# The edge stage of a graph network kernel by pairs of tiles, with ScalarE making the one-hots from distances

## The chip, the cores and the metric

One core of a Trainium2 chip runs the program. The metric is the device time of one execution in microseconds (us); lower is better. The kernel before was run three times in the series shown here, and one further execution was profiled.

## The reference, cut to what matters

```python
h = relu(layernorm(x))                       # x: 3125 nodes, 256 features
msg_input = concat([h[src], h[dst], edge_attr])   # 50000 edges, sorted by dst; 16 edge features
hid = relu(msg_input @ mW1 + mb1)            # 512 wide
messages = hid @ mW2 + mb2
aggregated = segment_sum(messages, src)      # per source node
x = x + h + (relu(concat([h, aggregated]) @ uW1 + ub1) @ uW2 + ub2)
# then three graph convolutions over the same edges, with degree norms and self loops
```

Since the sum over edges is linear, the kernel sums `hid` per source node first and multiplies by `mW2` afterwards. With A = h @ mW1[0:256] + mb1 and B = h @ mW1[256:512], the hidden row of an edge is relu(A[src] + B[dst] + edge_attr @ mW1[512:528]).

## The kernel before, in words

There are four stages with a barrier between them. `sort_and_embed` groups the edges by blocks of 128 source nodes and writes them to a list in DRAM (`src_list`), computes A (kept in SBUF, as an upper and a lower part of 512 columns a block) and B (written to DRAM). `edge_mlp` is the edge stage. `build_and_update` builds the count matrix C and updates the nodes, and `graph_layers` does the three convolutions.

The list is cut into NT = 440 tiles of 128 edges. Tiles come in PAIRS = 220 pairs; both tiles of a pair belong to one block of source nodes, so the sums of a pair go to one place. Each engine runs its own written-out loop in order, and semaphores connect them. For tile t of the edge stage:

- SyncE (line 937) loads the list's rows, four tiles at a time, into a ring of four such groups.
- GpSimd copies the indices of four tiles (line 946) and gathers the 128 rows of B of a tile with an indirect DMA (line 949), up to eight tiles ahead of VectorE's addition.
- VectorE makes the one-hot `oh` (line 1031): iota equal to the edge's source within the block, 128 wide, float32r.
- TensorE turns the one-hot and the edge features (`turn`, lines 963 and 964, bf16).
- ScalarE copies the turned one-hot to SBUF and sums it along the row into `tile_deg` (line 1009, with a read of the accumulator), and copies the turned edge features (line 1011).
- TensorE adds three products of 512 columns into PSUM (`edge`, lines 971 and 973): edge features times weights, and the turned one-hot times the two parts of A, which picks A[src]. Where A is read depends on the pair's block, whose offset comes from a register.
- VectorE adds the gathered rows of B (`pre`, line 1040).
- ScalarE applies relu (line 1018). An even tile is written in float32 as `hid_whole`. An odd tile is written in float32r as `hid_upper`, and VectorE makes the rest, `hid_lower` = max(pre, 0) - upper (line 1046).
- TensorE multiplies the one-hot into the pair's sum (`node`): line 987 for a whole tile, lines 983 and 985 for the upper and lower part of a split tile.
- VectorE adds the pair's result onto the sums of its block (line 1055), or begins new ones, with `going_on` as the factor.

TensorE's loop does turn(t), edge(t-1), node(t-3); ScalarE's turn copies of t, relu of t-1; VectorE's one-hot of t+1, addition of t-2, lower part of t-3 and, each second time, a pair's sum. The block offsets are loaded into registers (line 72) every four pairs, on TensorE and on VectorE, where the group has five values, as the sum also reads at the previous pair's offset. In `build_and_update`, the degree sums of 440 tiles are turned in four blocks of 128 (lines 1217 and 1318) and multiplied with weights `tile_w` that say to which block a tile belongs (line 1334).

## Time and profile before

| | us |
|---|---|
| median of three runs | 2326.61 (2321.5 to 2326.86) |
| the profiled execution, its own time | 2330.37 |
| its span, first to last instruction | 2328.6 |
| the edge stage in it | 684.0 to 1404.5 |

Busy times over the span are TensorE 1882.8 us (81%), VectorE 1575.9 (68%), GpSimd 1255.4 (54%) and ScalarE 823.2 (35%), and the mean granted clock of TensorE is 0.885 of full speed.

A busy time is the time in which an engine had an instruction in it; register, branch and semaphore instructions are not counted. PE is TensorE, PEld its weight load, DVE VectorE, ACT ScalarE, POOL GpSimd, SP SyncE; a q behind the name is the engine's sequencer. "idle before" is the time for which an engine stood still ahead of an instruction, with what released it; "issue" is time for which the profile shows no releaser. L1040 is line 1040 of the kernel before.

### The profile page before, as it was taken

How to read it: one execution, taken by the hardware profiler on the slowest of the kernel's cores; microseconds unless marked ns; L12 is line 12 of the kernel's file. 1: busy time of each engine (PE TensorE's matmuls, PEld its weight loads, DVE VectorE, ACT ScalarE, POOL GpSimd, SP SyncE). 2: the span in 40 equal slices, each digit the busy share in tenths (PEclk: the TensorE clock that was granted, in tenths of full speed). 3: DMA queues.
4: the chain of work that ended last, by engine and by line, in shares of the span. 5: the costliest groups of instructions: out<-in, count | busy, mean ns of one | idle time of the engine just before them, and what ended most of it. 6: DMA issues, size and time to landing. Idle time of an engine off the chain costs nothing. (4 is left out here: it accounts for less than half of the span.)

```text
span 2328.6 us, 36393 instructions
## 1 busy us (share of the span) xinstructions
PE 1882.8 (81%) x8866; PEld 1281.5 (55%) x8866; DVE 1575.9 (68%) x4877; ACT 823.2 (35%) x2533; POOL 1255.4 (54%) x1508
## 2 busy tenths in 40 slices
PE   3354656455448999999999998999997999999998
PEld 2222323232225555555555555777675788788786
DVE  7665656465448999999989997787777535335333
ACT  0111111111115666666666664555556012112000
POOL 3566665665656666666666656999887500000000
PEclk7576676666659999999999998999998999999999
DMA  4011111111126666666666684111115333333333
GB/s 137 26 41 37 39 44 35 41 33 42 34 65 173 183 180 180 183 180 181 186 171 184 184 161 129 61 59 59 59 64 152 94 109 115 103 109 120 97 109 96
DMA packets 179413, 247.68 MB, mean 106 GB/s; under 512 B 28860, under 2 KB 146937, under 8 KB 179210
## 3 DMA queue, kind: packets, MB, share of 16 engines
q0 software_dynamic: 47888, 126.25, 19.8%
q1 hardware_dynamic: 99730, 93.08, 13.2%
q10 hardware_dynamic: 31592, 26.02, 3.4%
q8 instruction: 81, 1.33, 0.2%
q14 instruction: 122, 1.00, 0.2%
HBM read 199.08 MB, written 46.09 MB: 105 GB/s over the span
## 5 line engine op out<-in xcount | busy, mean ns | idle before, releaser
L366 POOL DMA_INDIRECT src_list<-ring,ring_row x392 | 405.7, 1035 | 263.4 <-DVE ring L584 148.9
L949 POOL DMA_INDIRECT brow<-B_rows,rows x440 | 421.4, 958 | 230.6 <-DVE pre L1040 150.2
L1822 PE MATMUL pO<-F,y 128*128 128x512 f32 x1728 | 437.9, 407 | 10.7 <-DVE y L1642 6.5
L1822 PEld LDWEIGHTS pO<-F,y 128*128 128x128 f32 x1728 | 327.8, 190 | 90.4 <-DVE y L1642 6.8
L973 PE MATMUL pEdge<-A,turned 128*128 x880 | 362.7, 494 | 0.0
L1040 DVE TENSOR_TENSOR pre<-pEdge,brow 128x512 f32<-128x512 f32 x440 | 301.5, 685 | 44.1 <-PE pEdge L973 21.8
L1186 POOL TENSOR_SCALAR src_oh<-iota,src_s 128x128 bf16<-128x128 bf16 x473 | 303.2, 656 | 32.6 <-PE pC L1357 30.5
L791 PE MATMUL pP<-U,upto 128*128 128x182 bf16 x385 | 61.3, 327 | 296.8 <-DVE posf L554 292.3
L791 PEld LDWEIGHTS pP<-U,upto 128*128 128x128 bf16 x385 | 44.8, 130 | 335.2 <-DVE posf L554 312.4
L987 PE MATMUL pNode<-hid_whole,oh 128*128 128x512 f32 x440 | 229.1, 602 | 0.0
L1018 ACT ACTIVATE hid_upper<-pre 128x512 fp32r<-128x512 f32 x220 | 138.7, 631 | 243.2 <-DVE pre L1040 195.3
L1638 DVE CAST F<-raw 128x512 fp32r<-128x512 uint16 x432 | 173.7, 438 | 66.4 <-PE pO L1822 60.6
L971 PE MATMUL pEdge<-we_rows,turned_e 96*128 96x512 bf16 x440 | 170.7, 388 | 40.7 <-ACT turned_e L1011 34.7
L1230 DVE TENSOR_SCALAR dst_oh<-iota_cw,dst_s 128x458 bf16<-128x458 f16 x568 | 182.8, 374 | 0.7 <-PE pC L1357 0.4
L1055 DVE SCALAR_TENSOR_TENSOR sums<-sums,going_on,pNode 128x512 f32 x220 | 163.2, 742 | 27.1 <-issue 26.8
L973 PEld LDWEIGHTS pEdge<-A,turned 128*128 128x128 f32 x880 | 171.5, 195 | 11.9
L554 DVE CUSTOM_DVE_ANT_0 junk<-pP,U 128x182 bf16<-128x182 f32 x392 | 109.2, 339 | 100.6 <-remote 95.6
L1357 PE MATMUL pC<-dst_oh,src_oh 128*128 128x458 bf16 x568 | 157.6, 362 | 14.9 <-SPq L1304 6.0
L1046 DVE SCALAR_TENSOR_TENSOR hid_lower<-pre,hid_upper 128x512 fp32r<-128x512 f32 x220 | 149.8, 681 | 0.8 <-ACT hid_upper L1018 0.7
L1442 ACT CAST c_rows<-pC 128x458 uint16<-128x458 f32 x175 | 94.6, 541 | 155.6 <-PE pC L1357 138.7
L1018 ACT ACTIVATE hid_whole<-pre 128x512 f32<-128x512 f32 x220 | 139.2, 633 | 16.3 <-DVE pre L1040 5.5
L513 DVE TENSOR_SCALAR U<-bin_iota,bin_f 128x182 bf16<-128x182 bf16 x392 | 76.9, 284 | 89.8 <-remote 89.6
(284 smaller groups left out, 3257.2 us busy)
## 6 DMA issues: line engine op xcount, KB each, us to landing
raw<-C_rows SPq DMA_DIRECT2D x72, 768.0 KB, 4.4
C_rows<-c_rows ACTq DMA_DIRECT2D x175, 114.5 KB, 1.7
rows<-src_list SPq DMA_DIRECT2D x110, 100.0 KB
brow<-B_rows,rows POOLq DMA_INDIRECT x440
B_rows<-bst SPq DMA_DIRECT2D x25, 256.0 KB
src_list<-ring,ring_row POOLq DMA_INDIRECT x392
hT_rows<-A SPq DMA_DIRECT2D x25, 128.0 KB
resid<-in_x_dram SPq DMA_DIRECT2D x1, 3072.0 KB
```

The lines of the kernel that those rows point to most:

```text
L366: nc.gpsimd.indirect_dma_start(dr.src_list[:, :, :].rearrange("p t w -> (p t) w"), bass.IndirectOffsetOnAxis(ap=ring_row[:, k % RING, t:t ...
L949: nc.gpsimd.indirect_dma_start(brow[:, t % BR, :], None, dr.B, bass.IndirectOffsetOnAxis(ap=rows_i[:, b, j, 1:2], axis=0)).then_inc(b_in[t ...
L971: mm(pE[t % 2][:, :], turned_e[:, t % 2, :], keep.we[:, :], start=True, stop=False)
L973: last = mm(pE[t % 2][:, :], turned[:, t % 2, :], keep.A[:, 2 * HID + k * HID:][:, bass.ds(at[t // 2], HID)], start=False, stop=(k == 1))
L987: last = mm(pN[p % 2][:, :], oh[:, t % OHS, :].bitcast(F32), whole[(t % 4 + 1) // 2][:, :], start=first, stop=not first)
L1018: nc.scalar.activation(to, pre[:, u % 2, :], ACT.Relu).then_inc(hid_ready, 1)
L1040: v.tensor_tensor(pre[:, t % 2, :], pE[t % 2][:, :], brow[:, t % BR, :], ALU.add).then_inc(pre_ready, 1)
L1055: v.scalar_tensor_tensor(out=keep.sums[:, bass.ds(at[p], HID)], in0=keep.sums[:, bass.ds(at[max(p - 1, 0)], HID)], scalar=keep.going_on[:, ...
L1186: nc.gpsimd.tensor_scalar(src_oh[:, s % SLOTS, :], keep.iota16[:, :], src_s[:, s:s + 1], None, ALU.is_equal).then_inc(src_ready, 1)
L1230: v.tensor_scalar(dst_oh[:, s % SLOTS, :], iota_cw[:, :], dst_s[:, s:s + 1], None, ALU.is_equal).then_inc(dst_ready, 1)
L1638: v.tensor_copy(F[:, n % FS, :], raw[:, m % RAWS, n % RAWW, :]).then_inc(f_ready, 1)
L1822: last = mm(pO[m % 2][half][:, :], y[:, win, part, half * P:(half + 1) * P], F[:, n % FS, :], start=(win == 0 and part == 0), stop=False)
```

## The change

The edge stage goes by pairs. Each of TensorE's, ScalarE's and VectorE's steps handles two tiles.

- VectorE's one-hots are gone. ScalarE computes for each tile the distances |source - iota| (`distances`, Abs, bf16, 128 wide, two instructions a pair), two pairs ahead. From them it makes the one-hots of a pair as relu(1 - distance) in one instruction of 256 columns (`one_hots`). TensorE turns the distances rather than the one-hots, and ScalarE's copy of the turned ones applies relu(1 - distance) on the way (`turn_over`, 256 wide, its row sum going into `pair_deg`). The bias of Abs, and the one of both relus, is an operand of one value a partition.
- In every first (even) pair, as before, the first tile is whole and the second is split. In every second (odd) pair both tiles are split: ScalarE's upper and VectorE's lower part are then 1024 wide.
- VectorE's addition is one instruction of 1024 columns a pair, into a PSUM tile of two banks; SyncE and GpSimd wait for it by pairs.
- TensorE's loop does turn(i), edge(i-1), node(i-3) of pairs. node(p) waits for the sum of pair p-2 by `sums_ready`. ScalarE's does turn_over(i), distances(i+2), one_hots(i), relus(i-2); VectorE's add_target(i-1), lower_part(i-2), add_pair(i-4).
- The registers are loaded every eight pairs, eight values at a time, on both engines, on VectorE within add_pair.
- `build_and_update` has 220 degree sums, in two blocks, and computes the weights of pairs.
- The semaphores of the first stage's set-up are merged into one, `set_up`, in the order in which GpSimd counts it up.

The core of the diff; of the edge stage only the new lines and those that stay are shown:

```diff
...
+        LCS = 4
         BR = 8
+        GRP = 8
+        QUADS = NT // LC
+        OHR = 6
+        DR = 4
+        WHOLE, SPLIT = 2, 2
         rows = g.sb("rows", [P, LCS, LC, ROW])
         brow = g.sb("brow", [P, BR, HID])
+        apart = g.sb("apart", [P, DR, 2, P], BF16)
+        oh = g.sb("oh", [P, OHR, 2, P], F32R)
+        turned = g.sb("turned", [P, 2, 2 * P], F32R)
+        turned_e = g.sb("turned_e", [EW, 2, 2 * P], BF16)
+        pre = g.sb("pre", [P, 2, 2 * HID])
+        whole = g.sb("hid_whole", [P, WHOLE, HID])
+        upper = g.sb("hid_upper", [P, SPLIT, 2 * HID], F32R)
+        lower = g.sb("hid_lower", [P, SPLIT, 2 * HID], F32R)
         pT = [g.ps(f"pTurn{n}", [P, 2 * HID], BF16) for n in range(2)]
+        pE = [g.ps(f"pEdge{n}", [P, 2 * HID]) for n in range(2)]
         pN = [g.ps(f"pNode{n}", [P, HID]) for n in range(2)]
+        apart_ready = g.sem("apart_ready")
+        whole_ready = g.sem("whole_ready")
+        upper_ready = g.sem("upper_ready")
+        sums_ready = g.sem("sums_ready")
+        def both(p):
+            return p % 2 == 1
+        def first(p):
+            return 0 if both(p) else HID
+        def wholes(p):
+            return p - p // 2
         block = stack.enter_context(nc.Block())
         @block.sync
         def _(sp):
+            for m in range(QUADS):
                 if m >= LCS:
+                    sp.wait_ge(pre_ready, 2 * (m - LCS + 1))
                     sp.wait_ge(cols_copied, m - LCS + 1)
                 sp.dma_start(rows[:, m % LCS, :, :], dr.src_list[:, m * LC:(m + 1) * LC, :]
                              ).then_inc(rows_in[m % LCS], 16)
...
         @block.gpsimd
         def _(pool):
             for t in range(NT):
+                m, j = divmod(t, LC)
                 if j == 0:
+                    pool.wait_ge(rows_in[m % LCS], 16 * (m // LCS + 1))
+                    nc.gpsimd.tensor_copy(keep.cols[:, t:t + LC, :], rows[:, m % LCS, :, 0:2]).then_inc(cols_copied, 1)
                 if t >= BR:
+                    pool.wait_ge(pre_ready, (t - BR) // 2 + 1)
                 nc.gpsimd.indirect_dma_start(
                     brow[:, t % BR, :], None, dr.B,
+                    bass.IndirectOffsetOnAxis(ap=rows_i[:, m % LCS, j, 1:2], axis=0)).then_inc(b_in[t % BR], 16)
+            pool.wait_ge(cols_copied, QUADS)
         @block.tensor
         def _(pe):
             mm = nc.tensor.matmul
             at = blocks_of(nc, pe, keep.pair_at, 0, GRP)
+            def turn(p):
+                q, j = divmod(2 * p, LC)
+                pe.wait_ge(apart_ready, 2 * p + 2)
+                if p >= 2:
+                    pe.wait_ge(turn_copied, p - 1)
+                for n in range(2):
+                    nc.tensor.transpose(pT[p % 2][:, n * P:(n + 1) * P], apart[:, p % DR, n, :], keep.ident16[:, :])
+                for n in range(2):
+                    last = nc.tensor.transpose(pT[p % 2][0:EW, (2 + n) * P:(3 + n) * P],
+                                               rows16[:, q % LCS, j + n, 4:4 + EW], keep.ident16[:, :])
+                last.then_inc(turn_done, 1)
+            def edge(p):
+                pe.wait_ge(turn_copied, p + 1)
+                if p >= 2:
+                    pe.wait_ge(pre_ready, p - 1)
+                for n in range(2):
+                    to = pE[p % 2][:, n * HID:(n + 1) * HID]
+                    mm(to, turned_e[:, p % 2, n * P:(n + 1) * P], keep.we[:, :], start=True, stop=False)
+                    for k in range(2):
+                        last = mm(to, turned[:, p % 2, n * P:(n + 1) * P],
+                                  keep.A[:, 2 * HID + k * HID:][:, bass.ds(at[p], HID)], start=False, stop=(k == 1))
                 last.then_inc(edge_done, 1)
+            def node(p):
+                to = pN[p % 2][:, :]
+                pe.wait_ge(oh_ready, p + 1)
+                if p >= 2:
+                    pe.wait_ge(sums_ready, p)
+                if not both(p):
+                    pe.wait_ge(whole_ready, wholes(p) + 1)
+                    mm(to, oh[:, p % OHR, 0, :].bitcast(F32), whole[:, wholes(p) % WHOLE, :], start=True, stop=False)
+                pe.wait_ge(upper_ready, p + 1)
+                tiles = (0, 1) if both(p) else (1,)
+                for n in tiles:
+                    mm(to, oh[:, p % OHR, n, :], upper[:, p % SPLIT, n * HID:(n + 1) * HID],
+                       start=(both(p) and n == 0), stop=False)
+                pe.wait_ge(lower_ready, p + 1)
+                for n in tiles:
+                    last = mm(to, oh[:, p % OHR, n, :], lower[:, p % SPLIT, n * HID:(n + 1) * HID], start=False,
+                              stop=(n == 1))
                 last.then_inc(node_done, 1)
+            pe.wait_ge(sums_ready, 1)
+            for i in range(PAIRS + 3):
+                if i < PAIRS:
+                    turn(i)
+                if 0 <= i - 1 < PAIRS:
+                    edge(i - 1)
+                if 0 <= i - 3 < PAIRS:
+                    node(i - 3)
+                if i % GRP == 0 and 0 < i < PAIRS:
+                    at.update(blocks_of(nc, pe, keep.pair_at, i, min(GRP, PAIRS - i)))
         @block.scalar
         def _(act):
+            def distances(p):
+                q, j = divmod(2 * p, LC)
+                act.wait_ge(rows_in[q % LCS], 16 * (q // LCS + 1))
+                if p >= DR:
+                    act.wait_ge(turn_done, p - DR + 1)
+                    act.wait_ge(oh_ready, p - DR + 1)
+                for n in range(2):
+                    nc.scalar.activation(apart[:, p % DR, n, :], keep.iota[:, :], ACT.Abs,
+                                         bias=rows[:, q % LCS, j + n, 0:1], scale=-1.0).then_inc(apart_ready, 1)
+            def one_hots(p):
+                act.wait_ge(apart_ready, 2 * p + 2)
+                if p >= OHR:
+                    act.wait_ge(node_done, p - OHR + 1)
+                nc.scalar.activation(oh[:, p % OHR, :, :], apart[:, p % DR, :, :], ACT.Relu, bias=keep.ones[:, 0:1],
+                                     scale=-1.0).then_inc(oh_ready, 1)
+            def turn_over(p):
+                act.wait_ge(turn_done, p + 1)
+                if p >= 2:
+                    act.wait_ge(edge_done, p - 1)
+                nc.scalar.activation(turned[:, p % 2, :], pT[p % 2][:, 0:2 * P], ACT.Relu, bias=keep.ones[:, 0:1],
+                                     scale=-1.0, accum_out=keep.pair_deg[:, p:p + 1])
+                nc.scalar.copy(turned_e[:, p % 2, :], pT[p % 2][0:EW, 2 * P:4 * P]).then_inc(turn_copied, 1)
+            def relus(p):
+                act.wait_ge(pre_ready, p + 1)
+                if not both(p):
+                    if wholes(p) >= WHOLE:
+                        act.wait_ge(node_done, p - 2 * WHOLE + 1)
+                    nc.scalar.activation(whole[:, wholes(p) % WHOLE, :], pre[:, p % 2, 0:HID], ACT.Relu
+                                         ).then_inc(whole_ready, 1)
+                if p >= SPLIT:
+                    act.wait_ge(node_done, p - SPLIT + 1)
+                nc.scalar.activation(upper[:, p % SPLIT, first(p):2 * HID], pre[:, p % 2, first(p):2 * HID], ACT.Relu
+                                     ).then_inc(upper_ready, 1)
+            for p in range(2):
+                distances(p)
+            for i in range(PAIRS + 2):
+                if i < PAIRS:
+                    turn_over(i)
+                if i + 2 < PAIRS:
+                    distances(i + 2)
+                if i < PAIRS:
+                    one_hots(i)
+                if i >= 2:
+                    relus(i - 2)
         @block.vector
         def _(dve):
             v = nc.vector
+            v.memset(keep.sums[:, 0:HID], 0.0).then_inc(sums_ready, 1)
             at = {}
+            def add_target(p):
+                dve.wait_ge(edge_done, p + 1)
+                for t in (2 * p, 2 * p + 1):
+                    dve.wait_ge(b_in[t % BR], 16 * (t // BR + 1))
+                if p >= 2:
+                    dve.wait_ge(whole_ready, wholes(p - 1))
+                    dve.wait_ge(upper_ready, p - 1)
+                    dve.wait_ge(lower_ready, p - 1)
+                at_row = (2 * p) % BR
+                v.tensor_tensor(pre[:, p % 2, :], pE[p % 2][:, :],
+                                brow[:, at_row:at_row + 2, :].rearrange("p t n -> p (t n)"), ALU.add
+                                ).then_inc(pre_ready, 1)
+            def lower_part(p):
+                dve.wait_ge(upper_ready, p + 1)
+                if p >= SPLIT:
+                    dve.wait_ge(node_done, p - SPLIT + 1)
+                at_col = first(p)
+                v.scalar_tensor_tensor(out=lower[:, p % SPLIT, at_col:2 * HID], in0=pre[:, p % 2, at_col:2 * HID],
+                                       scalar=0.0, in1=upper[:, p % SPLIT, at_col:2 * HID].bitcast(F32), op0=ALU.max,
+                                       op1=ALU.subtract).then_inc(lower_ready, 1)
             def add_pair(p):
+                if p % GRP == 0:
+                    at.update(blocks_of(nc, dve, keep.pair_at, p, min(GRP, PAIRS - p)))
+                dve.wait_ge(node_done, p + 1)
+                dve.wait_ge(sums_ready, p + 1)
                 v.scalar_tensor_tensor(out=keep.sums[:, bass.ds(at[p], HID)],
                                        in0=keep.sums[:, bass.ds(at[max(p - 1, 0)], HID)],
                                        scalar=keep.going_on[:, p:p + 1], in1=pN[p % 2][:, :],
+                                       op0=ALU.mult, op1=ALU.add).then_inc(sums_ready, 1)
+            for i in range(PAIRS + 5):
+                if 0 <= i - 1 < PAIRS:
+                    add_target(i - 1)
+                if 0 <= i - 2 < PAIRS:
+                    lower_part(i - 2)
+                if 0 <= i - 4 < PAIRS:
+                    add_pair(i - 4)
+            dve.wait_ge(sums_ready, PAIRS + 1)
...
-            for m in range(KT):
-                link(v.tensor_scalar(ends_after[:, :], keep.tiles_end[:, 0:NW], part_m[:, m:m + 1], None, ALU.is_gt))
...
+            for m in range(KP):
+                link(v.tensor_scalar(pair_m[:, m:m + 1], keep.part[:, :], float(m * P), 2.0, ALU.add, ALU.mult))
+                link(v.tensor_scalar(ends_after[:, :], keep.tiles_end[:, 0:NW], pair_m[:, m:m + 1], None, ALU.is_gt))
+                v.tensor_copy(pair_w[:, m, 0:1], ends_after[:, 0:1]).then_inc(pair_w_ready, 1)
+                link(v.tensor_tensor(pair_w[:, m, 1:NW], ends_after[:, 1:NW], ends_after[:, 0:NW - 1], ALU.subtract))
...
+            for m in range(KP):
+                size = min(P, PAIRS - m * P)
+                last = mm(pX[:, 0:NW], degT[0:size, m, :], pair_w[0:size, m, :], start=(m == 0), stop=(m == KP - 1))
```

## Rows read from the trace of the kernel before

**Rows 1.** Busy time by stage: stretch, length, then each engine, clock, DMA share, GB/s
```profile
684.00:1404.50 720.50, 673.59 (x3080) 411.74 (x3080) 647.10 (x1321) 445.48 (x1760) 473.33 (x550) 0.98 0.64 177
```

**Rows 2.** The chain that ended last in order of time, first piece: start, us, what
```profile
1774.72 6.85 DMA raw<-C_rows
```

**Rows 3.** TensorE's order of time, one pair: start, us, engine, line, operation
```profile
1009.48 1.02 PE L987 MATMUL pNode<-hid_whole,oh 128*128 128x512 f32 x2
1010.33 0.22 PE L963 MATMUL pTurn<-ident,oh 128*128 128x128 bf16 x1
1010.39 0.22 PE L964 MATMUL pTurn<-ident,rows 128*96 128x128 bf16 x1
...
1011.13 0.39 PE L983 MATMUL pNode<-hid_upper,oh 128*128 128x512 f32 x1
...
1011.59 0.23 PE L963 MATMUL pTurn<-ident,oh 128*128 128x128 bf16 x1
```

**Rows 4.** The same view, whole node products at both ends of four pairs and between
```profile
1019.00 1.02 PE L987 MATMUL pNode<-hid_whole,oh 128*128 128x512 f32 x2
...
1025.03 1.05 PE L987 MATMUL pNode<-hid_whole,oh 128*128 128x512 f32 x2
...
1028.71 1.02 PE L987 MATMUL pNode<-hid_whole,oh 128*128 128x512 f32 x2
...
1031.64 1.02 PE L987 MATMUL pNode<-hid_whole,oh 128*128 128x512 f32 x2
```

**Rows 5.** VectorE's order of time, lower part and sum of two pairs
```profile
1007.17 0.68 DVE L1046 SCALAR_TENSOR_TENSOR hid_lower<-pre,hid_upper 128x512 fp32r<-128x512 f32 x1
1007.77 0.74 DVE L1055 SCALAR_TENSOR_TENSOR sums<-sums,going_on,pNode 128x512 f32 x1
...
1010.28 0.68 DVE L1046 SCALAR_TENSOR_TENSOR hid_lower<-pre,hid_upper 128x512 fp32r<-128x512 f32 x1
1011.45 0.75 DVE L1055 SCALAR_TENSOR_TENSOR sums<-sums,going_on,pNode 128x512 f32 x1 [0.49 <-issue]
```

**Rows 6.** VectorE's register loads, line 72, 1000 to 1050, then 684 to 702 us
```profile
L72 DVEq TENSOR_LOAD <-pair_at x4: 1180/1181/1183, 1010.0 to 1049.9; - x4
...
L72 DVEq TENSOR_LOAD <-pair_at x1: 594/594/594, 700.5 to 700.5; - x1
```

**Rows 7.** Groups by line and form, ScalarE then VectorE: busy us, mean ns, idle before
```profile
L1713 ACT ACTIVATE y<-h_g,dis 128x256 fp32r<-128x256 f32 x75 | 38.0, 509 | 21.6 <-PE pO L1822 19.6
...
L1747 ACT ACTIVATE h_g<-tmp 128x256 f32<-128x256 f32 x48 | 20.0, 416 | 132.9 <-DVE tmp L1664 132.9
...
L425 ACT ACT_TABLE_LOAD x1 | 1.3, 1283 | 0.0
...
L1257 DVE SCALAR_TENSOR_TENSOR sums<-mb,deg_src,pG 128x256 f32<-128x256 f32 x25 | 11.9, 475 | 7.9 <-PE pG L1367 7.9
```

**Rows 8.** ScalarE's order of time in the edge stage
```profile
1006.96 0.26 ACT L1009 ACTIVATE turned<-pTurn 128x128 fp32r<-128x128 bf16 x1
...
1007.21 0.25 ACT L1011 COPY turned_e<-pTurn 96x128 bf16<-96x128 bf16 x1
1007.36 0.63 ACT L1018 ACTIVATE hid_whole<-pre 128x512 f32<-128x512 f32 x1
1007.89 0.27 ACT L1009 ACTIVATE turned<-pTurn 128x128 fp32r<-128x128 bf16 x1
```

**Rows 9.** Groups by line, 700 to 1390 us: GpSimd's gathers
```profile
L949 POOL DMA_INDIRECT brow<-B_rows,rows x430 | 411.5, 957 | 228.0 <-DVE pre L1040 150.2 <-issue 77.8
```

**Rows 10.** All engines' order of time at the end of the stage
```profile
1402.11 0.69 DVE L1046 SCALAR_TENSOR_TENSOR hid_lower<-pre,hid_upper 128x512 fp32r<-128x512 f32 x1 [0.69 <-ACT hid_upper L1018]
...
1402.85 0.49 PE L985 MATMUL pNode<-hid_lower,oh 128*128 128x512 f32 x1 [0.23 <-DVE hid_lower L1046]
```

**Rows 11.** Groups by line, 1404 to 1425 us, VectorE then TensorE
```profile
L1217 DVE COPY degT<-pU 128x128 f32<-128x128 f32 (+1 forms) x4 | 0.9, 278 | 0.0
...
L1334 PE MATMUL pX<-tile_w,degT 128*128 128x25 f32 (+1 forms) x8 | 2.0, 392 | 1.7 <-DVE degT L1217 1.7
```

199 lines of the change are left out of this document (34 added, 165 removed).

## The prediction

> **What bounds the kernel now.** I first read the page and the busy times by stage: the change rewrites only the edge stage, from 684.0 to 1404.5 us, and there TensorE is busy 673.6, VectorE 647.1, GpSimd 473 and ScalarE 445 of 720.5 us [rows 1]. The chain of work that ended last starts at 1774.72 us [rows 2], after a barrier, so it says nothing of this stage; but all engines meet at its end, so what it gains or loses goes into the time in full. So I read its inner rhythm.
>
> TensorE's order of time is packed. The whole product takes 0.85 us (1009.48 to 1010.33), a tile's turn and edge products 0.80 (to 1011.13), the split product 0.46 (to 1011.59) [rows 3]. A pair is 2 x 0.80 + 0.85 + 0.46 = 2.91 us. From whole product to whole product one sees the real period: four pairs take 1031.64 - 1019.00 = 12.64 us, 3.16 a pair, where 4 x 2.91 is 11.64; of the 1.00 lost, 0.77 are in one pair, 1025.03 to 1028.71 [rows 4]. What lies there is VectorE's load of block offsets into registers: it takes 1.18 us, starting at 1010.0 in one group, and the sum behind it starts at 1011.45, 1.17 after the lower part's start, where a pair without a load has 0.60 (1007.17 to 1007.77) [rows 5, 6]. So TensorE is the bound, plus a hiccup each four pairs. The stage is 220 x 3.16 = 695.2 and 25.3 of start, end and rare stalls.
>
> **The change: what each engine has to do.** TensorE keeps four transposes and six edge matmuls a pair (2 x 0.80 = 1.60; each transpose takes 0.06 of it [rows 3]). Its node part is 0.85 + 0.46 = 1.31 in every first pair as now, and two split tiles, 0.92, in every second. Packed it would need 2.91 and 2.52, mean 2.72: the gain on offer is 0.19 x 220 = 42 us.
>
> VectorE loses its two one-hots (ScalarE makes them now), adds both targets in one instruction, and makes a lower part 1024 wide in every second pair. The slope is (0.74 - 0.475)/256 = 1.04 ns an element [rows 5, 7], so 512 more elements add 0.53: a 1024-wide one lets the next start after 1.13 us (bounds 1.06 and 1.20). Sum: 1.13 + (0.60 + 1.13)/2 + 0.74 = 2.74 us.
>
> ScalarE's present spacing is 0.25 for a 128-wide turn with its accumulator read, 0.15 for the edge features, and a 512-wide relu takes 0.63 and lets the next start after 0.53, 0.10 before its end [rows 8]. A 256-wide one with one pointer operand takes 0.509, without one 0.416: 0.093 for the pointer [rows 7]. The slope is (0.633 - 0.416)/256 = 0.85 ns. New, with a pointer in the first, third and fourth: turn 256 wide 0.25 + 0.11 + 0.09 = 0.45; features 0.15 + 0.11 = 0.26; two distances of 0.30; one-hots 0.41: 1.72 us. Relus: 0.53 + 0.53 in a first pair, 0.63 + 0.43 - 0.10 = 0.96 in a second. Mean 2.73 (bounds 2.5 without pointer cost, 2.9 with twice it).
>
> GpSimd is busy 473.3/220 = 2.15 us a pair [rows 1], and 77.8 us of gaps between its gathers, over some 215 pairs, wait for nothing that the profile shows [rows 9]: 0.36, together 2.51 at least. Its gathers keep eight tiles of lead and SyncE's loads of rows four groups of four; I cost both at nothing, covered while a pair takes over 2.5 to 2.7, and if that cover is gone VectorE's addition waits for gathers. Three engines are then within 0.02 of each other, and none bounds alone. The waits do.
>
> **The loop through the queues.** In ScalarE's new order the relus of pair i-2 stand behind the turn of pair i, though their input is long there. VectorE's lower part waits for them; the sum of pair i-4 is queued behind that lower part; TensorE's node product of pair i-2 waits for this sum (its PSUM bank); and the turn of pair i+2 is queued behind the node product. From turn i to turn i+2, pair i-2 a first (second) pair:
> - result visible 0.16 after the next could start (0.22 less 0.06 [rows 3]), start 0.02
> - ScalarE 1.72, then to the end of its upper part 0.53 + 0.63 = 1.16 (1.06)
> - to VectorE 0.05; lower part until the sum may start 0.60 (1.13); the sum 0.74 [rows 5]
> - to TensorE 0.05, as from 1402.11 + 0.69 to 1402.85, and 0.10 for weights that could not load ahead (0.49 against 0.39) [rows 3, 10]
> - node product 1.31 (0.92), turn 0.23
>
> That is 6.14 us (6.18) for two pairs, 3.08 a pair, over the packed 2.72: TensorE idles ahead of node products, and almost nothing of the 0.19 is left but what the hiccup gives back. VectorE fits in: it gets the edge result 1.56 after turn i, adds for 1.13, and is free at about 2.7 to 3.0, the lower part's inputs being there at 3.11.
>
> **The register loads.** VectorE's now come every eight pairs, of eight values instead of five. The first, of four, took 0.59 us and those of five 1.18 [rows 6], so they go by fours and eight cost 1.18 too. The load sits inside the loop: from its start to the sum is 1011.45 - 1010.0 = 1.45, against 0.60 [rows 5, 6]. That is 0.85 each eight pairs (bounds 0.3, if the other loop's idle absorbs it, and 1.5). TensorE's load stands behind a node product of 0.92 that hides it.
>
> Eight pairs: 4 x 6.14 + 0.85 = 25.4, 3.18 a pair; 220 x (3.18 - 3.16) = +4. Start and end: the first addition needs a second gather, +1.3, and the queues are a pair rather than a tile deep at the end, some +2 to +3; together I take +3 (bounds 0 and 6). The stage: 727.5.
>
> **The next stage** turns two blocks of degree sums, not four. Four copies take 0.9 and eight half matmuls 2.0 between the gathered columns and the first step [rows 11]; half goes: -1.4 (bounds 0 and -1.5). The longer building of the pair weights is hidden, as VectorE waits for TensorE's gathered columns behind it. The merged semaphores of the first stage change no order: nothing, as the same GpSimd instructions come first.
>
> Sum: +4 + 3 - 1.4 = +5.6 us. The profiled execution took 2330.4, so 2336; it stands 3.8 above the median 2326.6, by which I forecast 2332. About 0.3%, 7 us, is what a measurement of this kernel can tell from no change.
>
> **A rule against the change.** In VectorE's step the two one-hots are the rest of a pair: at 1.04 ns an element 128 are 0.13 and, with a start like the lower part's (0.60 - 0.53), 0.20 each [rows 5, 7]. ScalarE pays 0.30 x 2 + 0.41 for them, inside the loop [rows 7, 8]. The Trainium skill ("ScalarE: Activation LUTs", Rules for kernel authors) says that relu, max and add belong on VectorE. By that rule the loop would lose the 1.0 and be no bound (5.1), while VectorE's step grew to 3.14: again about today's time. The rows bear the rule out half: the move frees an engine that was not the bound and lengthens the one on the loop.
>
> **Rivals.**
> - The loop is shorter than I sum, or the waits overlap, and an engine's own work is the bound: 2.74 + 0.11 for the load = 2.85 a pair, 220 x 0.31 = 68 less: 2327 - 68 + 3 - 1 = 2261. For it: each engine's sum allows it, and each 0.1 off the loop gives 11 us. Against it: single steps of the trace start 0.03 to 0.05 after their release, so a sum of durations has held so far. Times between 2261 and 2318 belong here. Chance 0.25.
> - Slower: the eight-value load costs by the value. It is VectorE's load ahead of the sum, in the loop; five values in 1.18 make 0.236 each, eight 1.89, +0.71 each eight pairs, x 27.5 = +19.5: 2351. From a load of about 1.23 us up the result passes +0.3%. For: eight values were never loaded on VectorE here. Against: four took exactly half of five. Chance 0.15.
> - Slower by far: the distances' function is not in the table set that is active. A table load takes 1.283 us [rows 7]; two a pair bring ScalarE's own work to 2.73 + 2.57 = 5.3, 2.14 over today's pair, x 220 = +471: 2798. Against it: relu and copy alternate in this stage without one. Chance 0.02. The Trainium skill ("ScalarE: Activation LUTs", Table sets) says that abs, relu and copy are in every set, which speaks against it as well; no row here has an abs.
> - It does nothing: what bounds a pair lies outside the four queues, as GpSimd's gathers with waits that their lead does not cover, which the change leaves as they are: 2327. Chance 0.06.
>
> **How the numbers follow.** My forecast, 2332, has 0.52; its own range is 2318 to 2346, from 0.1 us on the loop either way (11 us) and the ends (3). It lies partly in each class: 0.10 faster, 0.22 same, 0.20 slower. Faster by over 0.3%: 0.25 + 0.10 = 0.35. Same: 0.22 + 0.06 = 0.28. Slower: 0.20 + 0.15 + 0.02 = 0.37. For 8 in 10 the range takes most of the first rival and all of the load's: 2280 to 2352, leaving out about 0.11 of the packed cases below, 0.02 of table loads and some 0.05 above.
>
> **What would show it.** Right: TensorE idle before node products, released by VectorE's sum, some 0.35 us a pair; ScalarE's relus never waiting for VectorE's addition; two pairs in about 6.15 us; a long pair each eight, with a load of 1.18. Each step can be seen by itself: distances 0.40 long, one-hots 0.51 (with the pointer), the upper part 1.06, lower part and addition 1.22, the stage near 727 us. Wrong: a pair at 2.8 to 2.9 with those waits absent, a load near 1.9, any table load in the stage, GpSimd busy without a gap with VectorE waiting for gathers, or TensorE's granted clock in the stage falling below the 0.98 [rows 1] it has now because of the idle stretches.

## The result, and the profile after

| | before | changed |
|---|---|---|
| median | 2326.12 us (2320.51 to 2335.12, 20 executions) | 2318.65 us (2306.74 to 2325.88, 20 executions) |
| profiled execution, its span | 2330.37, 2328.6 | 2321.22, 2319.4 |
| edge stage, first clearing of the sums to the end of the last sum | 684.0 to 1404.4: 720.4 | 680.9 to 1393.6: 712.7 |

The ratio is 0.9967, with an interval from 0.9955 to 0.998: 7.5 us faster. I had forecast 2332, slower than before by about as much. The value lies in the range; the direction is wrong.

The edge stage of the changed kernel as one window (columns as in [rows 1]: stretch, length, TensorE, its weight loads, VectorE, ScalarE, GpSimd, clock, DMA share, GB/s):

```profile
680.90:1393.60 712.70, 656.01 (x3080) 376.88 (x3080) 617.91 (x661) 608.23 (x1650) 573.28 (x550) 0.99 0.64 179
```

VectorE's instructions went from 1321 to 661 and its work barely changed (647.1 to 617.9); ScalarE's rose from 445.5 to 608.2. TensorE fell by 17.6 us, to 656.0 of 712.7 (the packed 2.72 a pair would be 598). Its clock held. GpSimd, for which I had costed nothing, rose from 473.3 to 573.3.

ScalarE's groups by form in the changed kernel (line, engine, operation, out<-in, count | busy us, mean ns | idle before, releaser):

```profile
L1021 ACT ACTIVATE apart<-iota,rows 128x128 bf16<-128x128 f32 x428 | 149.5, 401 | 0.0
L1048 ACT ACTIVATE hid_upper<-pre 128x1024 fp32r<-128x1024 f32 x107 | 112.3, 1050 | 0.0
L1028 ACT ACTIVATE oh<-apart,ones 128x256 fp32r<-128x256 bf16 x214 | 107.3, 501 | 0.0
L1035 ACT ACTIVATE turned<-pTurn,ones 128x256 fp32r<-128x256 bf16 x214 | 100.8, 471 | 93.0 <-PE pTurn L966 63.6 <-issue 24.4 <-remote 5.1
```

The single costs are those of the prediction: distances 0.401 (0.40 said), one-hots 0.501 (0.51), the wide upper part 1.050 (1.06). The idle column shows the loop: ScalarE never stands still ahead of a relu or a one-hot, only ahead of the turned distances.

The waits of the changed kernel, 700 to 1380 us (engine, line, waited for: us in total, times, longest):

```profile
PEld pNode L989 <- issue: 85.8, 106, 1.2
...
ACT turned L1035 <- PE pTurn L966: 63.6, 72, 2.3
...
DVE hid_lower L1087 <- ACT hid_upper L1048: 48.0, 144, 0.7
PE pNode L989 <- issue: 40.2, 101, 0.6
```

These are three places on the predicted loop: TensorE before the node product (no releaser is named; I had expected the sum to be), ScalarE for the turn behind it, VectorE's lower part for the relus. Of the 0.35 us a pair that TensorE was to idle ahead of node products, its own row shows 0.19 (40.2 over some 214 pairs). The pace fits too. Two sums eight pairs apart:

```profile
883.08 0.75 DVE L1096 SCALAR_TENSOR_TENSOR sums<-sums,going_on,pNode 128x512 f32 x1
...
908.45 0.75 DVE L1096 SCALAR_TENSOR_TENSOR sums<-sums,going_on,pNode 128x512 f32 x1
```

That is 25.37 us, and the other groups take 25.24 to 25.45 (the first 27.06, the last 24.02), where I had said 25.4. This agreement misleads, as the experiments show. What did not fit at once was the register load, of eight values in the changed kernel (min/median/max ns):

```profile
L73 DVEq TENSOR_LOAD <-pair_at x2: 597/600/603, 1008.9 to 1034.3; - x2
```

It takes 0.60 us. I had taken 1.18 [rows 6]. The kernel before has a row of four values on TensorE that neither the prediction nor its rows use:

```profile
L72 PEldq TENSOR_LOAD <-pair_at x4: 333/334/335, 1001.8 to 1039.7; - x4
```

The kernel before has stalls. From sum to sum its groups of four pairs take 12.63 to 12.66 us, except 17.57 (the first), 14.17, 14.57, 15.48, 13.28, 13.48 and 13.20. Less seven times 12.64 that is 13.3 us over the others. One of them, in ScalarE's, then VectorE's, then TensorE's order of time:

```profile
1042.27 0.63 ACT L1018 ACTIVATE hid_whole<-pre 128x512 f32<-128x512 f32 x1
1044.93 0.28 ACT L1009 ACTIVATE turned<-pTurn 128x128 fp32r<-128x128 bf16 x1 [2.03 <-PE pTurn L964]
```
```profile
1043.41 0.28 DVE L1031 TENSOR_SCALAR oh<-iota,rows 128x128 fp32r<-128x128 f32 x1
1044.98 0.69 DVE L1040 TENSOR_TENSOR pre<-pEdge,brow 128x512 f32<-128x512 f32 x1 [1.29 <-remote]
```
```profile
1043.53 0.22 PE L964 MATMUL pTurn<-ident,rows 128*96 128x128 bf16 x1
1045.50 0.39 PE L971 MATMUL pEdge<-we_rows,turned_e 96*128 96x512 bf16 x1 [1.76 <-ACT turned_e L1011]
```

The transpose is over at 1043.75, and ScalarE's copy and VectorE's addition start together 1.2 us later. Stalls of this size are absent from the middle of the changed kernel's stage. So I first held them to be the whole result: chance stalls of the profiled execution, which my sum had carried over inside "25.3 of start, end and rare stalls".

### The profile page after: what moved, and what is told of

Its sections match the earlier page's. It is cut to its first block and busy times, and to the rows that moved or that the text cites. A ratio compares the mean times of both kernels' runs of the same rounds, so it can differ in the third digit from the quotient of the medians.

```text
span 2319.4 us, 34772 instructions
## 1 busy us (share of the span) xinstructions
PE 1866.4 (80%) x8860; PEld 1245.8 (54%) x8860; DVE 1546.3 (67%) x4211; ACT 985.7 (42%) x2423; POOL 1354.1 (58%) x1508
## 3 DMA queue, kind: packets, MB, share of 16 engines
q8 instruction: 79, 1.29, 0.2%
## 5 line engine op out<-in xcount | busy, mean ns | idle before, releaser
L948 POOL DMA_INDIRECT brow<-B_rows,rows x440 | 450.3, 1023 | 122.8 <-issue 117.5
L978 PE MATMUL pEdge<-A,turned 128*128 x880 | 336.0, 493 | 0.0
L1078 DVE TENSOR_TENSOR pre<-pEdge,brow 128x1024 f32<-128x1024 f32 x220 | 268.6, 1221 | 34.6 <-PE pEdge L978 11.1
L1087 DVE SCALAR_TENSOR_TENSOR hid_lower<-pre,hid_upper 128x512 fp32r<-128x512 f32 x220 | 210.9, 959 | 55.4 <-ACT hid_upper L1048 48.0
L1048 ACT ACTIVATE hid_upper<-pre 128x512 fp32r<-128x512 f32 x220 | 183.7, 835 | 2.0 <-PE pNode L997 2.0
L993 PE MATMUL pNode<-hid_upper,oh 128*128 128x512 f32 x330 | 164.4, 552 | 2.9 <-issue 0.7
L1021 ACT ACTIVATE apart<-iota,rows 128x128 bf16<-128x128 f32 x440 | 153.6, 400 | 19.3 <-DMA rows<-src_list 19.3
L989 PE MATMUL pNode<-hid_whole,oh 128*128 128x512 f32 x220 | 121.3, 633 | 44.1 <-issue 41.5
```

The lines of the kernel that those rows point to most:

```text
L948: nc.gpsimd.indirect_dma_start(brow[:, t % BR, :], None, dr.B, bass.IndirectOffsetOnAxis(ap=rows_i[:, m % LCS, j, 1:2], axis=0)).then_inc( ...
L978: last = mm(to, turned[:, p % 2, n * P:(n + 1) * P], keep.A[:, 2 * HID + k * HID:][:, bass.ds(at[p], HID)], start=False, stop=(k == 1))
L993: mm(to, oh[:, p % OHR, n, :], upper[:, p % SPLIT, n * HID:(n + 1) * HID], start=(both(p) and n == 0), stop=False)
L1048: nc.scalar.activation(upper[:, p % SPLIT, first(p):2 * HID], pre[:, p % 2, first(p):2 * HID], ACT.Relu).then_inc(upper_ready, 1)
L1078: v.tensor_tensor(pre[:, p % 2, :], pE[p % 2][:, :], brow[:, at_row:at_row + 2, :].rearrange("p t n -> p (t n)"), ALU.add).then_inc(pre_re ...
L1087: v.scalar_tensor_tensor(out=lower[:, p % SPLIT, at_col:2 * HID], in0=pre[:, p % 2, at_col:2 * HID], scalar=0.0, in1=upper[:, p % SPLIT, a ...
```

## The experiments

The runs fell on four chips beside the first one. They are of two kinds, and the kernel before tells them apart: on two chips it takes 2204.6 to 2207.2 us, on the other two 2330 to 2354, like the first one's 2326. Below they are called **quick** and **long**, and the first chip is a long one. In the profiled executions the edge stage begins at 576 to 582 us on the quick ones and at 676 to 690 on the long ones, so most of the 120 us are gone before it.

| run | chips | time, before | ratio (95%) | eight pairs |
|---|---|---|---|---|
| before_again | quick | 2204.57, 2207.17 | one execution | 25.28 (2 x 12.64) |
| copy_on_vector | quick | 2198.85, 2207.17 | 0.9967 (0.9955 to 0.998) | 24.94 |
| relus_first | quick | 2172.1, 2207.17 | 0.984 (0.9823 to 0.9856) | 23.77 |
| both_moves | quick | 2177.48, 2207.17 | 0.9864 (0.9847 to 0.988) | 24.03 |
| after_again | long | 2335.21, 2353.93 | 0.9923 (0.9902 to 0.9945) | 25.4 to 26.3 |
| loads_of_four | long | 2329.65, 2353.93 | 0.9906 (0.9875 to 0.9936) | 24.9 to 26.4 |
| sum_first | long | 2365.94, 2353.93 | 1.0059 (1.0038 to 1.0081) | 26.0 to 28.2, mostly 26.9 |
| sum_relus_first | long | 2364.25, 2353.93 | 1.0065 (1.0042 to 1.0087) | 25.3 to 28.2, mostly 26.9 |
| sum_first_10 | long | 2364.11, 2351.56 | 1.0049 (1.0025 to 1.0073) | 25.5 to 28.2, mean 26.9 |
| relus_first_again | long | 2351.47, 2351.56 | 0.9989 (0.9967 to 1.0011) | 25.0 to 28.4 |
| relus_first_10 | long | 2326.75, 2351.56 | 0.9887 (0.9864 to 0.9911) | 24.2 to 26.2 |
| after_10 | long | 2323.74, 2351.56 | 0.9888 (0.9856 to 0.9919) | 24.97 |
| sum_first_half | quick | 2153.13, 2204.63 | 0.9763 (0.9735 to 0.9791) | 23.06 |
| relus_first_half | quick | 2170.18, 2204.63 | 0.984 (0.9812 to 0.9869) | 23.74 |
| after_half | quick | 2197.06, 2204.63 | 0.9963 (0.9947 to 0.9979) | 24.94 |
| before_half | quick | 2204.59, 2204.63 | 1.0 (0.9989 to 1.0011) | 25.28 |
| sum_first_again | long | 2318.58, 2329.97 | 0.9949 (0.9932 to 0.9967) | 23.7 to 27.0 |
| sum_first_half_again | long | 2311.14, 2329.97 | 0.9925 (0.9902 to 0.9949) | 23.5 to 26.4 |

The last column is the time from sum to sum eight pairs apart: one usual value, or the range without the first group and the last. The last two groups of relus_first, both_moves, relus_first_half and sum_first_half are longer than the value given (24.0 to 25.2, then 27.2 to 28.2).

Several expectations below were missed. Of relus_first, both_moves and sum_first I expected 22 to 23 us per eight pairs; after_again came out faster than either of its two cases (0.9923), after_half just under its 25.0, relus_first_10 above 0.980 to 0.987, and the last two runs between what the theories gave.

**relus_first** moves ScalarE's relus ahead of the distances. On the loop they then wait for 1.0 us less.

```diff
                 if i < PAIRS:
                     turn_over(i)
+                if i >= 2:
+                    relus(i - 2)
                 if i + 2 < PAIRS:
                     distances(i + 2)
                 if i < PAIRS:
                     one_hots(i)
-                if i >= 2:
-                    relus(i - 2)
```

> The changed kernel with one order altered: on ScalarE the relus of pair i-2 come directly behind the turn of pair i, ahead of the distances and the one-hots, which leaves 1.01 us (2 x 0.30 + 0.41) less of ScalarE's work in the loop of two pairs. Theory L (the loop turn, relus, lower part, sum, node product, turn sets the pace): the loop falls from 6.14 to 5.13 us, under TensorE's packed 5.44 for two pairs, so eight pairs go from 25.35 to some 22.2 to 23.2 us and the stage falls by 60 to 85 us; execution near 2245. Theory G (GpSimd sets the pace, since its four gathers and the copy take 6.2 to 6.5 us per two pairs in the changed kernel): eight pairs stay at 24.7 to 25.4, the stage falls by 0 to 18 us; execution 2300 to 2320. Both: the loop was first and GpSimd comes at once behind it; then 24.7, -18 us, with VectorE's additions now released by gathers.

23.77 us per eight pairs and 35 us less than before. The wait moved with the loop (the waits of relus_first, 620 to 1200 us):

```profile
DVE pre L1078 <- PE pEdge L978: 52.0, 98, 0.5
```

VectorE waits in every second pair for 0.53 us, ahead of the addition, where in the changed kernel ScalarE waits ahead of the turned distances. So the order of ScalarE's queue set the pace of the changed kernel, and a shorter loop, over the edge product, sets this one's: edge product to addition, lower part 1.13, sum 0.74, node product, turn, edge product. One turn of it in the trace starts at 900.39 (addition), 901.54, 902.67, 903.51, 904.52 and 904.76 (edge product), and two pairs take 5.94 us. I had expected TensorE's packed 5.44 to be next; this loop is longer. The cleanest comparison of the two orders is relus_first_half with after_half, on one chip: 2170.18 against 2197.06, 26.9 us.

**copy_on_vector** moves the copy of indices (1.14 to 1.23 us long on GpSimd in the changed kernel's profile) to VectorE; **both_moves** does this and relus_first.

```diff
-                    nc.gpsimd.tensor_copy(keep.cols[:, t:t + LC, :], rows[:, m % LCS, :, 0:2]).then_inc(cols_copied, 1)
...
+                if p % 2 == 0:
+                    m = p // 2
+                    v.tensor_copy(cols_as_i[:, m * LC:(m + 1) * LC, :], rows_i[:, m % LCS, :, 0:2]).then_inc(cols_copied, 1)
```

> The changed kernel with the copy of the tiles' index columns (1.13 us each two pairs on GpSimd) moved to VectorE, ahead of every second addition. Theory L: the loop is untouched except for some 0.1 us of VectorE's work ahead of the addition, which has 0.1 to 0.4 us to spare; eight pairs stay at 25.3 to 25.8 us, execution within 5 us of the changed kernel's. Theory G: GpSimd falls to about 5.1 us for two pairs, so the pace falls to what the loop or the engines allow, below 24.8 us for eight pairs; execution at least 15 us faster.

> Both edits together: relus ahead of distances and one-hots on ScalarE, and the index copy on VectorE. With the loop at 5.13 and GpSimd at 5.1 us for two pairs the bounds left are TensorE's packed 5.44, ScalarE's 5.5 and VectorE's 5.5 to 5.6 us. Theory L and theory G both expect 22.0 to 23.2 us for eight pairs and an execution near 2240 (2230 to 2260). If the loop alone was the bound, relus_first is already there and this adds under 5 us; if GpSimd stands directly behind the loop, this run is 50 us or more faster than relus_first.

The copy is worth nothing: 24.94 is also the pace of after_half, on the same kind of chip and with the copy on GpSimd; with relus_first it costs 0.26 per eight pairs. GpSimd was slower, but not the bound.

**before_again** is the kernel before, unchanged, for a second trace.

> The kernel before once more, unchanged, for one more trace. Its first trace had a strictly even period of 12.64 us for four pairs, but for stalls of 1.5 to 4.9 us at pairs 1, 53, 105, 157 and 210, which sum to 13 us and which the changed kernel's trace does not have. If these belong to the program, they return at the same pairs with about the same sum. If they are chance, they are elsewhere or gone, and the stage is then near 708 us.

12.63 to 12.66 us in every group but the first (12.92): the stage takes 702.4 us instead of 720.4. The program alone does not make the stalls. On a chip without stalls this leaves the changed kernel's gain unexplained, as the next ones show.

**after_again** is the changed kernel on a long chip, **loads_of_four** loads the offsets each four pairs.

```diff
-        GRP = 8
+        GRP = 4
```

> The changed kernel once more, unchanged, beside the runs of this chip. Expected from its first trace: 25.35 us for eight pairs again, no stalls in the stage, GpSimd's index copy at 1.1 to 1.2 us. The kernel before had 12.64 for four pairs and no stalls on this chip, so eight pairs differ by +0.07 us and the 220 pairs by +2; the start and end of the stage +3, the next stage -1.4, as in the forecast's sum, minus nothing for stalls: within 5 us of the kernel before if the stalls were the whole of the first result, ratio 1.000 to 1.003. If the gain belongs to the program (start and end of the stage, or the other stages), it returns: ratio near 0.997.

> The changed kernel with the block offsets loaded every four pairs, four values at a time, on VectorE and TensorE. Theory (a load goes by fours, 0.59 us each, and stands in the loop): the sum comes 0.59 + 0.27 = 0.86 after the lower part's start in place of 0.60, so +0.26 each four pairs, 0.52 for eight in place of 0.85: eight pairs 0.3 us shorter than the changed kernel's, about -9 us in all. Rival (the load's cost is hidden by the idle of the other pair's loop, or loads of eight cost by the value): no change, or up to 0.5 us longer for eight pairs.

The changed kernel has its own ragged groups there, 25.9 and 26.3 us beside 25.4, without one large stall. The loads of four values (TensorE's queue, then VectorE's):

```profile
L73 PEldq TENSOR_LOAD <-pair_at x4: 333/336/337, 1002.7 to 1041.1; - x4
L73 DVEq TENSOR_LOAD <-pair_at x4: 340/343/345, 1004.3 to 1043.4; - x4
```

Four cost 0.34 and eight 0.60. The two runs' intervals overlap, so whether GRP = 4 gains is open.

**sum_first** and **sum_relus_first** put VectorE's sum ahead of its lower part, the second with relus_first's order too.

```diff
                     add_target(i - 1)
+                if 0 <= i - 4 < PAIRS:
+                    add_pair(i - 4)
                 if 0 <= i - 2 < PAIRS:
                     lower_part(i - 2)
-                if 0 <= i - 4 < PAIRS:
-                    add_pair(i - 4)
```

> The changed kernel with VectorE's order altered: the sum of pair i-4 comes ahead of the lower part of pair i-2, so TensorE's node product no longer waits for a sum that stands behind a lower part, and only the products of the lower part wait for ScalarE's relus. Theory L: both loops (over ScalarE, 6.14 to 6.18 us for two pairs, and over the edge products, 5.73 to 5.87) lose the sum or the lower part and fall to about 5.4; what is left are TensorE's packed 5.44, ScalarE's 5.46 and VectorE's 5.3 to 5.5: eight pairs 21.8 to 22.8 us, the stage 70 to 95 us shorter than the changed kernel's. Theory G (GpSimd next, at 4 x 1.25 us and the copy of 0.4 to 1.2): eight pairs 21.6 to 24.7, with additions released by gathers. If neither holds and the pace is ScalarE's order, it stays at 25.3.

> Both orders altered: sum ahead of lower part on VectorE, relus ahead of distances and one-hots on ScalarE. Theory L: with the sum off the loops the ScalarE order has nothing left to give, so it is within 0.5 us of sum_first for eight pairs (21.8 to 22.5). If relus_first's 23.77 came from ScalarE's or GpSimd's own work and not from the loop over the edge products (5.87 us for two pairs, 23.5 for eight), this run stays at 23.5 to 23.8.

Both slower than before. For long stretches every fourth addition stands still for 2 us, each 13.4 us anew:

```profile
861.89 1.23 DVE L1078 TENSOR_TENSOR pre<-pEdge,brow 128x1024 f32<-128x1024 f32 x1 [2.07 <-remote]
...
875.33 1.22 DVE L1078 TENSOR_TENSOR pre<-pEdge,brow 128x1024 f32<-128x1024 f32 x1 [2.05 <-remote]
...
888.76 1.23 DVE L1078 TENSOR_TENSOR pre<-pEdge,brow 128x1024 f32<-128x1024 f32 x1 [2.04 <-remote]
```

"remote" names no engine, and eight gather buffers are four pairs, so I suspected late gathers. The next four tested it: ten buffers (paid for with one less of one-hots, distances and whole tiles) in three orders, and relus_first as it was.

```diff
-        BR = 8
+        BR = 10
...
-        OHR = 6
-        DR = 4
-        WHOLE, SPLIT = 2, 2
+        OHR = 5
+        DR = 3
+        WHOLE, SPLIT = 1, 2
```

> VectorE's order of sum_first with ten gather buffers in place of eight (the space comes from one buffer less of whole-rectified tiles, one less of one-hots and one less of distances). Theory G (on the chip of sum_first the gathers land about 9.7 us after they are issued, and the addition that frees two buffers, the two gathers behind it and their landing make a loop: 1.23 + .27 + .94 + .30 + .95 + 9.7 = 13.4 us for four pairs, which is the measured 26.87 per eight): with ten buffers the loop holds five pairs, 2.69 us a pair, and no longer decides; the 2.05 us wait of every fourth addition goes, eight pairs take 22 to 24 us and the time is 25 to 60 us below that of before on the same chip. Rival P (the wait has to do with TensorE or with the order of VectorE's queue, not with a gather): every fourth addition still waits, 26.9 us per eight pairs and a time above before's by .6%. If the chip is one on which gathers land after 4 us, both give the fast pace and the run says only that the order is not slow by itself.

> The same kernel as relus_first, here for another chip. Theory G: with a period of 23.8 us per eight pairs it would ask the gather loop of four pairs for 11.9 us, which a landing of 9.7 us does not allow (13.4): on a chip with the late landings it is held at 26 to 27 us per eight pairs and is no faster than before (ratio 1.000 to 1.008), on a chip with landings of about 4 us it repeats 0.984. Rival (the order alone sets the pace): .982 to .987 on any chip.

> relus_first with ten gather buffers. Theory G: 23.7 to 24.2 us per eight pairs on either kind of chip, ratio .980 to .987, so on a chip with late landings 1.5 to 2% under relus_first_again, on the other kind the same as it. Rival P: no difference from relus_first_again on any chip. This is the version that should beat both kernels wherever it runs.

> The changed kernel with ten gather buffers. Theory G: at 25.4 us per eight pairs it sits below what the late landings allow, so that part of its groups of 25.9 and 26.3 us on such a chip are the gathers' doing: with ten buffers they go, 25.4 throughout, 5 to 12 us less than the changed kernel's own time on such a chip (ratio to before .988 to .992). Rival: the loop through the queues alone sets it, with the same groups as before and a ratio of .992 to .997.

The theory of late landings fell: sum_first_10 has the same pace and the same waits, and in sum_first the landings themselves are on record, 3.3 to 6.5 us after the issue (median 3.6, of the 128 gathers with a full record) and not 9.7. But relus_first_again loses all of its gain on a long chip, as that theory had said, and ten buffers bring back most of it (0.9887); and the changed kernel with ten buffers runs at 24.93 to 25.02 us per eight pairs in 23 groups on end, without a ragged one (its first takes 32.1). What was left was the rate of the transfers. Of the last six, all but sum_first_again bring half the bytes: each gather fetches 128 rows of 256 columns in place of 512 (the other half of the buffers is zero, so half of the target's product is left out).

```diff
-                    brow[:, t % BR, :], None, dr.B,
+                    brow[:, t % BR, 0:HID // 2], None, dr.B_half,
```

> sum_first with gathers of half the bytes: each of the 440 gathers brings 256 of the 512 columns of 128 rows (128 KB in place of 256), the other half of each buffer holds zeros, so half of the target's product is left out. Every wait and every instruction stays. Theory D (gathers are held by the rate of the transfers): the 2.05 us waits of every fourth addition go, 22 to 23.5 us per eight pairs. Rival P (the waits come from TensorE and the queues' order): 26.9 us per eight pairs as before, with the same waits of the addition.

> relus_first with gathers of half the bytes, as above. Theory D: 23.5 to 24.0 us per eight pairs on any chip, without groups above 24.5. Rival P: 25 to 28 us on the chip on which relus_first had them.

> The changed kernel with gathers of half the bytes, as above. If its loop through the queues is its bound (as the prediction had it): 25.0 to 25.4 us per eight pairs, and no groups of 25.9 or 26.3. If transfers set its pace: under 24.8 us.

> The kernel before with gathers of half the bytes, as above. If its steady pace is TensorE's and its queues': 12.63 us per four pairs and no stalls above 13 us between (theory D puts the stalls down to the transfers). Rival P: stalls of 1 to 3 us in some places as in the first profile. If transfers set its pace too: under 12.5 us.

> The kernel of sum_first once more. On a chip whose first stage is long (before at 2320 us or more): 26.9 us per eight pairs and a ratio of 1.004 to 1.008, as before. On a chip whose first stage is short (before near 2205): theory D, with transfers that keep up there, 23.0 to 23.5 us per eight pairs and a ratio of .976 to .980; if whole gathers hold it there too, over 24.

> The kernel of sum_first_half on the same chip as sum_first_again. On a chip with the long first stage: theory D 23.0 to 23.5 us per eight pairs (ratio .975 to .980); rival P 26 to 27 us (ratio above 1.0). On a chip with the short one: 23.06 us as in sum_first_half.

The rate fell as well. On a long chip half the bytes leave sum_first as ragged as before (groups of 23.5 to 26.4, mean 25.1, against 25.2 with whole gathers), although the transfers move 99 GB/s instead of 182. On the quick chips relus_first does not care for them either (23.77, 23.74). And in sum_first the transfer engines have nothing to do just behind a stalled addition; 14 us from 866 in 40 slices, busy tenths and GB/s:

```profile
DMA  3848859293838588756697797649551000047663
GB/s 129 129 70 351 320 169 143 82 375 152 117 105 328 199 140 164 304 187 117 140 357 269 182 152 211 258 152 222 187 234 59 0 0 0 0 70 152 269 258 70
```

The zeros lie at 876.9 to 878.2, 2.4 us after the last gather was issued (874.49), so nothing is queued up.

What releases these waits can be read from the trace's record of semaphore updates. "remote" only says that no instruction ended near the update. The stalled addition of 875.33 waits for its two gathers, whose recorded landings end at 866.82 and 868.00, and for its edge product:

| TensorE's update | last instruction ends | recorded update |
|---|---|---|
| edge product | 873.26 | 875.31 |
| node product | 874.57 | 875.37 |
| turn | 874.81 | 875.43 |

The addition starts 0.02 us behind the first of the three. They come in one burst, though 1.5 us lie between their ends, while no recorded update of VectorE, ScalarE or GpSimd is late in this stage, on any chip. It is the same in all of the large waits: of the 55 waits of the addition over 0.9 us in sum_first (pairs 8 to 212), 54 end within 0.06 us of the update of TensorE's edge product, and in all 55 the last recorded landing of the addition's own gathers lies at least 5 us back. All five such waits in the kernel before end so too; the stall at 1044.98 has its updates at 1044.85, 1044.91 and 1044.96. In no trace of a quick chip does a TensorE update of these pairs come more than 0.1 us behind its instruction; on the long ones 34 do in the kernel before, 37 and 49 in the changed one (after, after_again), 179 in sum_first, and only 2 in after_10. So the stalls of the long chips are late updates of TensorE, and neither gathers nor transfers. Why the updates are late, why only there, and why more in some orders of the queues, stays open. The long chips' records also have gaps (310 of the 612 updates in the changed kernel, all 612 on quick chips), so these are counts of what was recorded.

## Why the prediction was wrong

after_half and before_half give what no other pair does: both kernels on one chip, with no stall in either. The rows of the first clearing and of the sums (first and last start), before_half, then after_half:

```profile
L1024 DVE MEMSET sums<- x1: 485/485/485, 581.8 to 581.8; 128x512 f32 x1
L1056 DVE SCALAR_TENSOR_TENSOR sums<-sums,going_on,pNode x220: 732/744/750, 592.1 to 1281.1; 128x512 f32 x110
```
```profile
L1067 DVE MEMSET sums<- x1: 485/485/485, 581.9 to 581.9; 128x512 f32 x1
L1097 DVE SCALAR_TENSOR_TENSOR sums<-sums,going_on,pNode x220: 734/742/749, 596.6 to 1273.9; 128x512 f32 x110
```

The stages take 700.0 and 692.7 us: 7.3 less, and the medians of the two differ by 7.5 (the two profiled spans by 5.8). The stage of the first chip's two traces is 7.7 shorter. Half the bytes do not disturb this: before_half stands to the kernel before at 1.0, and 24.94 is copy_on_vector's pace with whole gathers. By the terms of my sum:

| term | forecast | measured |
|---|---|---|
| steady pace, 27.5 groups of eight pairs | +4 (25.4 against 25.28) | -9.4 (24.94 against 25.28) |
| start and end of the stage | +3 | +2.0 (692.7 - 685.9 = 6.8, against 700.0 - 695.2 = 4.8) |
| next stage, from the edge stage's end to the first `pO` of the convolutions | -1.4 | -0.4 (376.25, against 376.65) |

- **The failed step is "The register loads"**: "they go by fours and eight cost 1.18 too". Eight cost 0.60 and four 0.34, so the 1.18 of the kernel before's five is no step from four to more. What makes five dear, their number or a start that is no multiple of it, was not tried. TensorE's load of four in the kernel before, 0.334 (the row above), could have told. The 0.59 that I took for the price of four was the stage's first load, and the first is dearer in every trace (min/median/max ns on VectorE, from the stage's start; fours in loads_of_four, then eights in the changed kernel):

```profile
L73 DVEq TENSOR_LOAD <-pair_at x4: 341/344/604, 708.3 to 748.0; - x4
```
```profile
L73 DVEq TENSOR_LOAD <-pair_at x3: 597/601/857, 703.0 to 755.6; - x3
```

So "four took exactly half of five" compared a first load with later ones, and did so by chance. With 0.60 the long pair costs 0.27 instead of 0.85, eight pairs 4 x 6.14 + 0.27 = 24.83, and the sum 5.6 - 27.5 x 0.58 = -10.4: 2316 in place of 2332, on the right side (measured: 2318.65). The rival by the value had the right shape (0.064 us a value between four and eight) and the wrong size and sign, as I priced it from the five.
- **The loop through the queues** was right, shown three times: by its length, by the waits above, and by relus_first, which shortens only it. In after_half two pairs take 6.18 us from one even pair's sum to the next, forecast as 6.14 and 6.18, and 6.40 where the loads lie, 0.22 more: 3 x 6.18 + 6.40 = 24.94. The packed-engines rival (2261) fell with it. The nearest to it is sum_first_half, with another order: 23.06, or 2.88 a pair, against its 2.85.
- **25.4 measured as 25.36** is no confirmation. It is 24.94 and 0.42 of what the long chips add to the groups of this kernel, 11.6 us over the stage. Most of it lies in one place: in the fifth pair of each group TensorE's update of the turn is recorded 0.35 us late (25 times), and the step from the sixth sum to the seventh takes 3.29 us instead of 2.95.
- **"25.3 of start, end and rare stalls"** was carried over as if it were the program's. It is 4.8 of the program's and 20.4 of the chip's. It did no harm by luck: the changed kernel's trace has 712.7 - 692.7 = 20.0 of the same. In the kernel before some 7.4 of it lie ahead of the first sum and 13.3 in seven stalls; in the changed one 8.5 lie ahead of the first sum and the rest in the groups. That the stalls had gone was my first explanation of the result, and it falls by before_half, which has none and is slower by the same 7.5.
- **The next stage**: two copies and four matmuls went, and in the quick pair VectorE's first one-hot comes 13.0 us behind the edge stage in place of 15.3 (on the first chip 14.1 in place of 15.0, with a wait of 1.1 us for the DMA of `ub`). But this does not reach the end: at the first `pO` 0.4 is left, and from the edge stage's end to the last instruction the changed kernel takes 1.4 us more (922.3 against 920.9; on the first chip 925.8 against 924.2). What takes it back is not known; these are single executions.
- **The first stage** began and ended the same in the quick pair; the 3.1 us by which it was shorter on the first chip lies within the scatter between long chips (676 to 690 us).
- **GpSimd costed at nothing** held for the time, though not for the load. It was costed as covered while a pair takes over 2.5 to 2.7 us, and no run came to that: the quickest, sum_first_half, takes 2.88. At the end of the stage the cover is thin, though: in relus_first the last gathers land 7.7 us after their issue instead of 4.0, VectorE's additions wait up to 1.6 us, and the last two groups take 24.9 and 28.2 in place of 23.8.
- **The rule against the change**: the Trainium skill ("ScalarE: Activation LUTs", Rules for kernel authors) puts relu, max and add on VectorE. Half of it can be answered here: the place of the one-hots in the queue is what lengthened the loop (26.9 us between relus_first_half and after_half). Behind the relus they cost the loop nothing (relus_first), and ScalarE has the time: 608.2/220 = 2.76 us a pair of work in the 2.97 that relus_first takes. No run has the one-hots of pairs on VectorE, so what the move by itself costs or gives is not shown.

**A version that beats both** is relus_first on quick chips (0.984, against 0.9963 of after_half) and relus_first_10 or after_10 on long ones (0.9887 and 0.9888, against 0.9923 of after_again in another series). relus_first_10 was not tried on a quick chip. sum_first_half shows what a third order could give, but sum_first with whole gathers was never on a quick chip.

## What to carry to other kernels

Where several engines run written-out loops, sum the loop through their queues, and then look for the instruction in it that nobody waits for: putting the relus ahead of the distances gave 27 us with two lines (2197.06 to 2170.18 on one chip). Price a small instruction from the row that has its shape, on any engine, before the row that has its name, and not from the first of its kind in a stage; an error of 0.6 us in a loop that turns 27 times decided the sign. Read the period of a stage from many groups and not as its length over its count, look at a second execution before rare stalls are booked to either kernel, and do not take a total that fits for a proof of its parts.

## What the runs showed of the hardware

- A register load on VectorE or TensorE takes 0.34 us for four values and 0.60 for eight, in groups that start at a multiple of their size; the first of a stage takes 0.52 to 0.60 and 0.78 to 0.86; five values, on VectorE in the kernel before, take 1.18.
- GpSimd's copy of 128 x 8 values takes 0.19 to 0.20 us in sum_first and after_10, 0.36 in relus_first, 0.49 in the kernel before and 1.14 to 1.23 in the changed kernel: it depends on what runs beside it. after_again has both cases in one trace: 71 copies that start beside VectorE's 1.22 us lower part, which reads SBUF twice, take 1.14 to 1.29, and 24 beside its equally long addition, which reads PSUM and SBUF, take 0.19 to 0.21. The mean gather on GpSimd goes from 0.96 (before) to 1.23 (after_10), and not together with the copy, which takes 0.20 in after_10.
- On the long chips TensorE's semaphore updates come up to 2.5 us late and in bursts (875.31, 875.37 and 875.43 for ends at 873.26, 874.57 and 874.81), which the waits view calls "remote" or "issue".
- Chips differ in more than a factor. The kernel before is 5% quicker on some, nearly all of it in the first stage; but the same kernel gains 1.6% over it on one and nothing on another (relus_first 0.984, relus_first_again 0.9989), and sum_first turns from 0.9949 to 1.0059 between two long chips. A kernel that is tuned on one chip only may be tuned to it.
- The granted clock of TensorE was 1.00 from 620 to 1200 us in relus_first and 0.97 from 720 to 1380 in sum_first and relus_first_again, where the waits are long: it was lower where TensorE idled more, and cannot explain the stalls themselves, at 1.00 from 866 to 882 us in sum_first.
